# Edge counts from tiles sorted by source block, in a graph network kernel on one core

## What is computed

```python
def _rgcn_conv(x, weight, root, bias, src, dst, etype):
    out = x @ root + bias
    for r in range(4):
        sel = etype == r
        deg = zeros(n).at[dst].add(sel)
        norm = where(sel, 1 / maximum(deg[dst], 1), 0)
        h_r = x @ weight[r]
        out = out + segment_sum(h_r[src] * norm[:, None], dst, n)
    return out

x = relu(rgcn(x, ..1)); x = relu(rgcn(x, ..2)); x = rgcn(x, ..3)
```

## Time and profile before

| what | us |
|---|---|
| median of three runs (lowest, highest) | 1761.36 (1759.18, 1761.56) |
| the profiled execution, own time | 1763.69 |
| its span, first to last instruction | 1761.9 |
| TensorE matmul busy | 1577.8 (90%) |
| TensorE weight load busy | 1447.7 (82%) |
| VectorE busy | 884.7 (50%) |
| ScalarE busy | 396.2 (22%) |
| GpSimd busy | 503.1 (29%) |
| L1467 matmuls, 1620 of them | 226.2 |

### The profile page before, as it was taken

How to read it: one execution, slowest core, us unless ns; L and a number is a source line. 1 busy time by engine, 2 the same in 40 slices (tenths; PEclk the granted TensorE clock), 3 DMA queues, 4 the chain that set the end, 5 groups by cost and what they waited for, 6 DMA issues and landing times.

```text
span 1761.9 us, 25506 instructions
## 1 busy us (share of the span) xinstructions
PE 1577.8 (90%) x9198; PEld 1447.7 (82%) x9198; DVE 884.7 (50%) x2013; ACT 396.2 (22%) x698; POOL 503.1 (29%) x560
## 2 busy tenths in 40 slices
PE   4999998999999999999999999897859958688864
PEld 2667678999999999999999899897759828687842
DVE  7887765541232132322232435555775255798643
ACT  1000022200111101111110211435532413466221
POOL 6100002233444343333444322245034371100300
PEclk9999998999999999999999999898979988788867
DMA  3000000111111221111111211231003201000001
GB/s 122 19 1 0 1 1 23 32 55 54 54 54 55 85 63 41 50 50 54 54 54 55 58 41 36 92 104 50 1 5 117 76 0 58 14 1 1 27 1 44
DMA packets 47625, 75.05 MB, mean 43 GB/s; under 512 B 5261, under 2 KB 43149, under 8 KB 47399
## 3 DMA queue, kind: packets, MB, share of 16 engines
q1 hardware_dynamic: 45184, 66.02, 12.7%
q10 hardware_dynamic: 2340, 7.68, 1.2%
HBM read 71.76 MB, written 1.92 MB: 42 GB/s over the span
## 4 chain that ended last, share of the span: by engine, by line
PE 77%; DVE 14%; issue 3%; DMA 2%; ACT 2%; POOL 0%; DVEq 0%; ACTq 0%; SPq 0%; PEldq 0%
PE psum L1467 12%; PE psum L1407 11%; PE psum L1410 11%; PE psum L1411 11%; PE psum L1424 7%; PE psum L1427 7%; PE psum L1766 6%; PE psum L1695 3%; PE psum L1699 2%; PE psum L1700 2%; DVE max_scratch L1207 2%; PE psum L1711 2%; DVE probs L1231 1%; DVE ln_stats L955 1%; PE psum L1396 1%
## 5 line engine op out<-in xcount | busy, mean ns | idle before, releaser
L1407 PE MATMUL psum<-w_lo,xT_hi 128*125 128x384 f32 (+1 forms) x1110 | 380.5, 343 | 1.8 <-DVE xT_lo L794 1.2
L1410 PE MATMUL psum<-w_hi,xT_lo 128*125 128x384 f32 (+1 forms) x1110 | 376.5, 339 | 0.0
L1411 PE MATMUL psum<-w_hi,xT_hi 128*125 128x384 f32 (+1 forms) x1110 | 376.1, 339 | 0.0
L497 POOL CAST w_hi<-w_raw 128x384 fp32r<-128x384 f32 x210 | 109.2, 520 | 748.2 <-PE psum L1411 733.7
L870 DVE TENSOR_TENSOR h_lo<-psum,h_hi 125x384 fp32r<-125x384 f32 (+1 forms) x120 | 66.9, 557 | 393.2 <-ACT h_hi L577 393.1
L1467 PE MATMUL psum<-onehot_dst,onehot_src 125*125 125x512 bf16 (+2 forms) x1620 | 226.2, 303 | 7.0 <-DVE onehot_dst L852 5.4
L499 POOL TENSOR_TENSOR w_lo<-w_raw,w_hi 128x384 fp32r<-128x384 f32 x210 | 217.6, 1036 | 16.8
L1467 PEld LDWEIGHTS psum<-onehot_dst,onehot_src 125*125 125x125 bf16 (+1 forms) x1620 | 157.6, 138 | 75.4 <-DVE onehot_dst L852 5.9
L1407 PEld LDWEIGHTS psum<-w_lo,xT_hi 128*125 128x125 f32 (+1 forms) x1110 | 208.3, 188 | 3.0 <-DVE xT_lo L794 1.5
L1410 PEld LDWEIGHTS psum<-w_hi,xT_lo 128*125 128x125 f32 (+1 forms) x1110 | 208.3, 188 | 0.3
L1411 PEld LDWEIGHTS psum<-w_hi,xT_hi 128*125 128x125 f32 (+1 forms) x1110 | 207.8, 187 | 0.0
(11 more groups left out here) (194 smaller groups left out, 2169.8 us busy)
## 6 DMA issues: line engine op xcount, KB each, us to landing
w_raw<-weights_dram SPq DMA_DIRECT2D x296, 192.0 KB, 2.4
x_nat<-x_dram SPq DMA_DIRECT2D x1, 1875.0 KB
x_residual<-x_dram SPq DMA_DIRECT2D x1, 1875.0 KB
out_dram<-x_residual SPq DMA_DIRECT2D x5, 375.0 KB
rgcn_bias<-rgcn_bias_dram SPq DMA_DIRECT2D x1, 1125.0 KB
par<-L_gnn_a_src_dram ACTq DMA_DIRECT2D x3, 375.0 KB
par0b<-L_gnn_a_dst_dram ACTq DMA_DIRECT2D x3, 375.0 KB
par<-L_gnn_b_dram ACTq DMA_DIRECT2D x3, 375.0 KB
```

The lines of the kernel that those rows point to most:

```text
L497: nc.gpsimd.tensor_copy(mem.wh[:, slot, :], mem.raw[:, raw_slot, :]).then_inc(w_hi_ready, 1)
L1407: ins = nc.tensor.matmul(o, h, wl, start=(j == 0), stop=False, skip_group_check=True)
L1410: nc.tensor.matmul(o, l, wh, start=False, stop=False, skip_group_check=True)
L1411: ins = nc.tensor.matmul(o, h, wh, start=False, stop=stop and j == k - 1, skip_group_check=True)
```

## The change

1. **Sorting on chip.** VectorE marks which source block each edge is in, TensorE ranks the edges in their block (`count_blocks`), and 80 permutation steps put each edge in a sorted place: a tile holds 128 edges of one block. Each step is three VectorE operations (`perm` 128 wide, `goal` twice 84 wide) and one matmul of 168 columns. A block takes as many tiles as it needs; 84 are made. `place_tiles` writes each tile's block number, and `sorted_edges` the sorted values.
2. **Two matmuls a tile.** The source one-hot is now 125 wide and made once for both pairs. The product goes to bank `block`, whose address TensorE holds in a register; registers are loaded in 8 groups of 21. The 114-column tails lie in banks 5 and 6. Four sweeps of 42 tiles (two pairs, two halves), ring of ten. Seven matmuls at each sweep's start write a middle value.
3. **Counts as int16.** ScalarE rounds the packed sum to get the odd relation, one multiply-add on VectorE gives the even one. The tables are no longer cleared as a whole. The last decode stands beside the first three products.
4. **Layer 0's ten root products** go in the edge phase, two beside the permutation and eight in the sweeps, by bank 7, with their weights first in the stream. The bias is added later by VectorE. Layer 0 ends with its last sums and then the transposes.
5. **Degrees** come from two columns of ones beside h in layer 0's first half (386 columns, `HX`), read after each relation; the 20 products of `degrees` go.

```diff
+SNAP = 1.5 * 2 ** 23
-OH_RING = 6
+OH_RING = 10
+        def adjacency_plan():
+            out, roots = [], [(f, m) for f in range(2) for m in range(NB)]
+            for t in range(ET):
+                out.append(("perm", t))
+                if t in (23, 31, 39, 47, 55):
+                    out.append(("turn", (t - 23) // 8))
+                if t in (67, 75):
+                    out.append(("root",) + roots.pop(0))
+            for s in range(SWEEPS):
+                for t in range(GROUP):
+                    out.append(("tile", s, t))
+                    if t % 12 == 9 and t < 36 and roots:
+                        out.append(("root",) + roots.pop(0))
+                    if s and t >= 14 and t % 5 == 4 and (t - 14) // 5 < NB:
+                        out.append(("odd", s - 1, (t - 14) // 5))
+                out.append(("sweep", s))
+            out += [("odd", SWEEPS - 1, m) for m in range(NB)]
+            return out
...
-            nc.gpsimd.memset(mem.sweep[:, 1, :, :], 0).then_inc(decoded, 1)
-            for r in (2, 3, 0, 1):
-                nc.gpsimd.memset(mem.cnt[:, r, :, :], 0.0).then_inc(zeroed, 1)
+            for r in range(NREL):
+                nc.gpsimd.memset(mem.cnt[:, r, NB - 1, :], 0)
...
+            def permute(t):
+                nc.vector.tensor_scalar(mem.perm[0:BP, slot, :], mem.iota[0:BP, 0:128], mem.slot_f[0:BP, t:t + 1],
+                                        None, ALU.is_equal)
+                for k, data in enumerate((mem.dst_f, mem.code_f)):
+                    ins = nc.vector.tensor_scalar(mem.goal[0:BP, slot, k * BLOCK_TILES:(k + 1) * BLOCK_TILES],
+                                                  mem.iota[0:BP, 0:BLOCK_TILES], mem.tile_f[0:BP, t:t + 1],
+                                                  data[0:BP, t:t + 1], ALU.is_equal, ALU.mult)
...
+            def onehots(s, t):
+                if s % 2 == 0:
+                    nc.vector.tensor_scalar(mem.oh_src[:, t, 0:BP], mem.iota[:, 0:BP], mem.s_src[:, j:j + 1],
+                                            mem.s_val[:, j:j + 1], ALU.is_equal, ALU.mult)
+                nc.vector.tensor_scalar(mem.oh_dst[:, n % OH_RING, 0:N], mem.iota[:, 0:N], mem.dst_pair[:, s % 2, j:j + 1],
+                                        None, ALU.is_equal).then_inc(onehot_ready, 1)
...
+                if q == 0:
+                    nc.vector.scalar_tensor_tensor(e_all, o_all, -float(BASE), v, ALU.mult, ALU.add).then_inc(decoded, 1)
                 else:
+                    link(nc.vector.scalar_tensor_tensor(e, o, -float(BASE), v, ALU.mult, ALU.add))
+                    nc.vector.scalar_tensor_tensor(e_all, e, 2.0 * MIDDLE, e_all, ALU.add, ALU.add)
+                    nc.vector.scalar_tensor_tensor(o_all, o, 2.0 * MIDDLE, o_all, ALU.add, ALU.add).then_inc(decoded, 1)
...
+            def tile_sums(s, t):
+                if t == 0:
+                    begin_sweep(s)
+                if t % (GROUP // 2) == 0:
+                    pe.wait_ge(place_ready, 1)
+                    j = s // 2 * GROUP + t
+                    places[:] = nc.values_load_multi_w_load_instructions(
+                        mem.place_i[0:1, j:j + GROUP // 2], engines=[mybir.EngineType.PE], min_val=0,
+                        max_val=128 * (NB - 1))[1]
+                n, v = s * GROUP + t, places[t % (GROUP // 2)]
+                pe.wait_ge(onehot_ready, n + 1)
+                for w, o in ((0, ps[0:BP, bass.ds(v * 4, 512)]), (512, ps[0:BP, bass.ds(v + NB * 512, TAIL)])):
+                    ins = nc.tensor.matmul(o, mem.oh_src[:, t, 0:BP], mem.oh_dst[:, n % OH_RING, w:w + 512 if w == 0 else NC],
+                                           start=False, stop=(t == GROUP - 1), skip_group_check=True)
...
-            for l in range(RLAYERS):
-                relations(l, 0, first=1 if l else 0)
+            relations(0, 0)
+            relations(0, 1)
+            agg(0, 1, H_UNITS - 1)
+            for m in range(NB):
+                pe.wait_ge(out_read, OUT_L - NB + (NB if m == 3 else m + 1))
+                turn(KC, of(mem.xn), UNITS, m, FIRST_BANKS)
```

More of the change, by code:

```diff
@@ L320, in program @@
         TAIL = NC - 512
-        SWEEP_BANKS = [(5, 512, NC), (6, 512, NC)] + [(m, 0, 512) for m in range(NB)]
+        SWEEPS = 4
+        READS = NB + 2
+        PER_SWEEP = NB
         MASK_HALVES = ((0, 3 * BP), (3 * BP, N))
@@ new lines, in _ @@
+            dve.wait_ge(consts_ready, 4)
+            for step in plan:
+                if step[0] == "perm":
+                    permute(step[1])
+                    if step[1] == ET - 1:
+                        place_tiles()
+                        sorted_edges()
+                elif step[0] == "turn":
+                    turn_lo(0, KC, mem.xh, mem.xl, False, step[1])
+                elif step[0] == "tile":
+                    onehots(*step[1:])
+                elif step[0] == "odd" and step[1] < SWEEPS - 1:
+                    decode(*step[1:])
@@ L1391, in turn @@
                     q = 2 * m + i
[L1392 to L1393 removed]
+                    used = [p for p in range(q) if turn_bank(p, banks) == turn_bank(q, banks)]
+                    if used:
+                        pe.wait_ge(xT_lo_ready, u0 + used[-1] + 1)
                     b = turn_bank(q, banks) * 512
@@ new lines, in begin_sweep @@
+            def begin_sweep(s):
+                pe.wait_ge(onehot_ready, s * GROUP + 1)
+                pe.wait_ge(consts_ready, 4)
+                if s:
+                    pe.wait_ge(sweep_read, s * READS)
+                else:
+                    pe.wait_ge(xT_lo_ready, UNITS)
+                for b in range(NB + 2):
+                    w = TAIL if b == 6 else 512
+                    nc.tensor.matmul(bank(b, 0, w), mem.init_rows[0:2, :], mem.init_cols[0:2, 0:w], start=True, stop=False,
+                                     skip_group_check=True)
@@ new lines, in _ @@
+            count_blocks()
+            for step in plan:
+                if step[0] == "perm":
+                    permute(step[1])
+                elif step[0] == "turn":
+                    if step[1] == 0:
+                        pe.wait_ge(x_loaded, 16)
+                    turn(KC, of(mem.xn), 0, step[1])
+                elif step[0] == "root":
+                    early(*step[1:])
+                elif step[0] == "tile":
+                    tile_sums(*step[1:])
+            pe.wait_ge(sweep_read, SWEEPS * READS)
@@ L1827, in weight_stream @@
         w, root = i["L0_gnn_W" + layer], i["L0_gnn_root" + layer]
+        rel = [w[r] for r in range(NREL)]
+        if layer == "1":
+            chunks += lay_chunks([(root, PIECES)])
         for piece in PIECES:
-            for m in [w[r] for r in range(NREL)] + [root]:
+            for m in rel if layer == "1" else rel + [root]:
                 chunks += lay_chunks([(m, [piece])])
```

576 lines of the change are left out of this document (347 added, 229 removed).

## The result

The changed kernel takes 1773.07 us (median of four; 1769.04 to 1776.68), the one before 1761.24 beside it: a ratio of 1.0069, 95% interval 1.0045 to 1.0093. It is slower by 12 us, where 63 us less were forecast. The profiled execution took 1776.7 us, 3.6 above the median; the one before was 2.3 above its own.

A forecast was written before the change was run, and what follows sets the result against it. TensorE was taken to bound both the edge phase and the dense phase behind it. Gains of 33.9 us up to the third product and 29.5 in layer 0 made 63.4 off 1761.4: 1698 us, range 1640 to 1758.

The forecast's parts named there:

- part 2: The four sweeps up to the last tile: 139.6 us, from tiles 55.4, root products 25.2, register loads 54 and clock 5.
- Part 1: Up to the first one-hot tile, with preparation, permutation, transposes and sorted lists: 95 us, where the pair ends at 30.2 before.
- Part 2, tile cost: TensorE's two matmuls a tile in the sweeps, with places from registers: 0.33 us each, 168 tiles making 55.4 us.
- rival C: In the sweeps TensorE's sequencer is the bound at 0.5 us a tile: 28 us more, 1726; 15 in 100.
- Part 2, load cost: Eight register-load groups on TensorE's queue: 8.0 us each (4.8 checks, 3.2 load), 64 in all, 54 of it counted.
- Part 2, the bank reading: ScalarE empties seven banks at each sweep's start, 3.94 us, taken to lie beside the 8.0 us group load.
- Part 2, the clock: Eight gaps in TensorE's work in the sweeps, each costing 0.6 us of slow clock: 5 us.
- rival E: Gaps and thin permutation keep TensorE at 1.2 GHz for half of the sweeps: 35 us more, 1733; 7 in 100.
- Rival A: Register loads in the sweeps cost 17.9 us a group, each value its own round: 79 us more, 1777; 8 in 100.
- Rival B: Loads nearly free, at most 1 us a group; VectorE and bank reading bound the sweeps at 104 us: 1662; 20 in 100.
- Part 3: From the last tile to the third product: 17.2 us, including about 4 of waiting before the over-row product; 24.3 before.
- Part 4: Layer 0: ten root products leave the dense phase, 31.5 us, less 2 of ScalarE and VectorE steps: 29.5 us gained.

## Why the prediction was wrong

The forecast was 1698 us, faster; it is 1773, slower, and outside the range. The direction failed by part 2, in four of its steps: the load was mis-sized, a wait by the order of ScalarE's queue was missing, the bank reading was counted as covered, and the slow clock was put at 5 us. Step by step:

- **Part 1** was right: 95 forecast, 90.1 measured. The permutation step (0.60), the 2 us of the second root product and the sorted lists (5.1 us, 5.6 forecast) were of the size worked out. Two errors went opposite ways. VectorE is ready to permute at 14.7 us and not 12.0; the casts still wait, for 3 us, while GpSimd's smaller memsets run. Beside GpSimd's splits a step takes 1.56 us, so three operations get in for two of GpSimd's, where one for one was assumed: some 8 us lost, 14 forecast.
- **Part 2, tile cost**: rival C is refuted. The register arithmetic on TensorE is 0.046 us for each matmul, not what VectorE's loop had suggested, and the sequencer hands on the 20 matmuls of ten tiles in 2.4 us. Twelve tiles in a row take 3.30 us (24 matmuls from 125.6 us on), the 137 ns each of the kernel before, so the 0.33 us a tile was too much, by 9 us in all.
- **Part 2, load cost**: the term was mis-sized. 8.0 us a group were forecast (4.8 checks, 3.2 load), 11.1 and 7.7 measured (5.9 checks; 4.98 or 1.6 load). The rows of the one load gave 0.19 + 0.03 for a check; from start to start it is 0.28, with time between the records too. The load proved to depend on the start address, which no row of before could show. The figure quoted there from the Trainium skill ("Runtime: NRT & Kernel Launch"; it stands in the section Instruction fetch mechanics) is about 200 ns a register, for loads from HBM. These loads are from SBUF: those off the multiple of 16 are near it (4.98 us by 21 is 0.237), the others far below (0.077).
- **Part 2, cover**: of 64 us of loads 54 were counted; of 81 real ones TensorE stood idle for 68.8, and the run without them gave back 74. The matmuls still queued covered about as little as assumed.
- **Part 2, the order**: this step is missing. The text asked what is queued behind the waiting load on TensorE's own engine, and went on to VectorE's ring, but not to ScalarE's queue, where the reading of the root product stands ahead of the rounding. It is worth 26 us. The plan in the diff held all that was needed to see it.
- **Part 2, the bank reading**: it was counted as lying beside the group load, and is not: 10.0 us of TensorE's waits, three times 3.3. That too could be read in the diff, where `begin_sweep` stands ahead of the load.
- **Part 2, the clock**: 5 us were set, a granted 0.70 was measured over 214 us. At the full clock the matmuls of the sweeps are 46 us of tiles, 25 of root products and some 6 of initial ones (an estimate from 0.1375, 0.175 and 0.22 us each), 77 in all; TensorE is busy for 114.6. So about 37 us are slow matmuls, which is the size of rival E (35). What the whole would gain from the full clock is not shown, since no run changes the clock alone. When the waits go the clock rises too (0.70, then 0.82, then 0.89), so part of each gain above is the clock's.
- **Part 2, the sum**: TensorE's own time accounts for the 74 us. Against the forecast it is busy 29 us longer (114.6, where 80.6 and 5 were set), idle 15 longer for the loads (68.8, not 54), and waits 19 for one-hots and 10 for the bank reading, both set at nothing.
- **Rival A** forecast 1777, but by 17.9 us a group. The time is near it by accident: the groups took 11, and order, bank reading and clock made the rest. Rival B was half right: with loads of 1.6 us, no checks and the new order it is 1686, not 1662.
- **Part 3**: 17.2 us forecast, 14.4 measured. The 4 us of waiting in it came later and were 8.3. Without them 13.2 were forecast; the first product went by at the slow clock.
- **Part 4**: 29.5 forecast, 18.9 measured. Of the 10.6 that are missing 8.3 are the late counts. The run with the earlier decode got 9 us back, and with them the clock: 0.87 in the changed kernel from 318 to 345 us, 1.00 there. "Idle time of TensorE in layer 0 over 6 us" was one of the forecast's own signs of being wrong.
- **Range**: its upper end took in dearer loads, or the sequencer and the clock, never loads and clock together, and nothing for a wait not thought of. The parts' errors are +74 and +11 us against -5 and -3. That the large ones have one sign is no accident: behind the waits for a load matmuls ran at 0.32 us and not 0.17.

## What to carry to other kernels

A step moved to "idle" time of one engine brings its readers and their places in other queues with it: for each moved product, write down what stands behind its reader on every engine, and put it where nothing urgent does. Cutting TensorE's matmuls in the sweeps from 1620 to 364 is worth nothing when its sequencer stops eight times for 8 to 11 us; count sequencer time like engine time, and loads of values known by construction need no checks. After such a change ask which engine's lead was counted as cover, and what consumes it first. A wait and a load are not side by side because both stand at the same place: look which comes first in that engine's queue.

## What the runs showed of the hardware

- A load of 21 values from SBUF to registers took 1.61 to 1.81 us where the list started at a multiple of 16 bytes, else 4.98 us (lists 8, 24, 20 and 28 bytes past a multiple of 32 all took that), on TensorE's sequencer.
- A bounds check of one loaded value took 0.28 us of it (records of 0.146 and 0.018), so 21 took 5.9 us, more than the load. Without the 168 checks the kernel took 47 us less.
- While its sequencer loaded and checked, TensorE got nothing: it ran dry 1.8 us after the load began in the group at 108.7, and waited for 9.3 us.
- A matmul into a PSUM address held in a register took 0.046 us of register arithmetic and no visible time of TensorE: 24 such matmuls in a row took 3.30 us, 0.1375 each, and 0.137 with fixed addresses in the kernel before.
